# Half of the head pairs in swapped key order: three turnings instead of four per half, a mixing in smaller tiles, and the deviation put on the values by GpSimd

## The reference, cut to what matters

```python
h = tok(x)                                   # (128, 128, 128)
q, k, v = (layernorm(h) @ w + b for each)    # 8 heads of 64
logits = q @ k.T / 8, masked: key <= query   # 128 queries, 128 keys
h = h + softmax(logits) @ v @ wo + bo
h = h + routed_ffn(layernorm(h))             # top 2 of 8 experts
```

## Time and profile before

| | |
|---|---|
| median of 3 runs | 1257.07 us (1255.15 to 1257.45) |
| the profiled execution: its own time | 1256.33 us |
| its span from first to last instruction | 1254.6 us |
| work outside the span (1256.33 - 1254.6) | 1.7 us |
| busy: PE, DVE, ACT, POOL | 93%, 79%, 79%, 60% of the span |

### The profile page before, as it was taken

One profiled execution on the slowest core, in us unless ns is written; L12 is line 12 of the kernel. 1 busy time (PEld: TensorE's weight loads), 2 busy tenths in 40 slices (PEclk: granted clock), 3 DMA queues, 4 the chain that ended last, 5 costly groups with the idle time before them and its releaser, 6 DMA issues. The chain is left out here.

```text
span 1254.6 us, 45360 instructions
## 1 busy us (share of the span) xinstructions
PE 1172.8 (93%) x13125; PEld 1031.4 (82%) x13126; DVE 993.3 (79%) x3799; ACT 992.7 (79%) x3491; POOL 755.2 (60%) x1082
## 2 busy tenths in 40 slices
PE   6899999999999999999999999729999997999996
PEld 4578888888888888888888887619999996999995
DVE  6568988888888888888888887756777774777774
ACT  2799999999999999999999998726666664666663
POOL 6436755565565555565565555544777774777775
PEclk9899999999999999999999999968999998999998
DMA  5151110100100111110010111115666663555552
GB/s 177 60 186 56 39 35 32 43 32 32 47 32 32 43 36 32 42 37 32 32 43 32 36 43 40 53 53 170 197 206 199 203 191 130 159 143 143 159 153 68
DMA packets 68049, 108.97 MB, mean 87 GB/s; under 512 B 12756, under 2 KB 32948, under 8 KB 67860
## 3 DMA queue, kind: packets, MB, share of 16 engines
q1 hardware_dynamic: 50068, 62.67, 17.7%
q0 software_dynamic: 17920, 45.55, 10.0%
HBM read 45.66 MB, written 54.11 MB: 80 GB/s over the span
## 5 line engine op out<-in xcount | busy, mean ns | idle before, releaser
L764 ACT ACTIVATE probs<-ps,neg_max 128x128 f32<-128x128 f32 (+1 forms) x1024 | 337.8, 363 | 2.0 <-DVE neg_max L961 1.9
L764 ACT ACTIVATION_READ_ACCUMULATOR probs<-ps,neg_max 128x1 f32 x1024 | 236.3, 231 | 0.0
L574 POOL TENSOR_TENSOR probs<-probs,inv_sums 128x384 f32<-128x384 f32 x120 | 99.2, 826 | 205.4 <-DVE inv_sums L910 205.4
L1143 DVE SCALAR_TENSOR_TENSOR probsT<-ps,b_now,masked 128x256 f32<-128x256 f32 x286 | 125.3, 480 | 85.5 <-PE ps L1237 66.0
L1235 PE MATMUL ps<-xT_hi,w_now 128*128 128x256 f32 x572 | 173.1, 303 | 0.8 <-DVE xT_lo L1127 0.8
L720 ACT ACTIVATE masked<-ps,b_now 128x256 f32<-128x256 f32 x286 | 119.8, 471 | 59.5 <-PE ps L1237 59.1
L1237 PE MATMUL ps<-xT_hi,w_now 128*128 128x256 f32 x572 | 162.8, 285 | 0.0
L1236 PE MATMUL ps<-xT_lo,w_now 128*128 128x256 f32 x572 | 161.9, 283 | 0.0
L631 POOL DMA_INDIRECT xs<-normed,row x128 | 137.0, 1070 | 41.2 <-issue 36.9
L1418 PE MATMUL ps<-w,probsT 128*128 x1144 | 150.8, 275 | 0.0
L1363 PEld LDWEIGHTS ps<-probsT,v 128*64 128x64 f32 x2048 | 109.8, 137 | 45.2 <-issue 44.4
(11 more groups left out here) (243 smaller groups left out, 3181.8 us busy)
## 6 DMA issues: line engine op xcount, KB each, us to landing
v<-xs SPq DMA_DIRECT2D x108, 260.0 KB
kT<-xs SPq DMA_DIRECT2D x35, 260.0 KB
xs<-pad_rows SPq DMA_DIRECT2D x16, 520.0 KB, 3.4
normed<-h SPq DMA_DIRECT2D x32, 256.0 KB, 2.6
w_parts<-in_w SPq DMA_DIRECT2D x1, 2048.0 KB, 8.9
xs<-normed,row POOLq DMA_INDIRECT x128, 2.7
xs<-v POOLq DMA_INDIRECT x108
out_h<-v POOLq DMA_INDIRECT x108
```

Source lines behind the costliest of these rows:

```text
L764: ins = nc.scalar.activation(probs_p[par][:, half, slots[n]], ps[:, SCORES + half, slots[n]], ACT.Exp, bias=neg_max[par][:, half, n:n + 1] ...
L1143: V.scalar_tensor_tensor(actT[z][:, f], ps[:, H2[z], f * BLK:(f + 1) * BLK], b1_now[j % WBUFS][:, 2 + f:3 + f], gate[z][:, f], ALU.add, AL ...
```

## The change

1. `key`: ACT stores the keys of the odd pairs of heads with the two halves of each sequence exchanged (a negative step over halves in its read).
2. `scores`, `max`, `exp`: same number of products and columns; `slots` are moved, so that of a half's 384 columns every 128 are one full 128 x 128 block. The lower queries of an even pair sit beside those of an odd pair, whose lower keys are now "upper" ones: the one fills partitions 0 to 63, the other 64 to 127 after turning.
3. `probsT0`, `probsT1`: three turnings of 128 x 128 a half in place of four, and copies of 384 columns in place of 512, without a scale. `probsT1` gets a wait for `mixT_ready`, as its bank is now used by the mixing too. The zeros of L1149 are gone.
4. `mix`: 16 products of 64 columns: first 8 for the lower queries in tiles of 64 rows by 64 columns, then 8 for the upper ones in tiles of 128 rows by 64 columns; into two banks (3 and 4). ACT's copy reads both banks.
5. `value` (and the table for it, once): the odd pairs' values must stand in exchanged order too, so that the one product of 512 columns becomes one of 256 columns and two of 256 columns whose outputs are 64 partitions each.
6. A new step `vscale` on POOL multiplies the values of one sequence (128 x 512) in place by 1/deviation. DVE puts the exchanged copy of `rstd` beside it with two small copies at the end of `norm`. `rstd_now` and its copy are gone. The first mixing of a group waits for `v_scaled` in place of `v_ready`.

```diff
@@ octet_steps
         if octets_done == 0 and k == 0:
             steps.extend(("value", 0, n) for n in range(GB))
+            steps.extend(("vscale", 0, n) for n in range(GB))
...
             late("route_weight", half - 2)
+        steps.append(("vscale", half + 1, n))
         late("scatter", half - 3, n, n + 1)
@@ final_steps
-        steps += [*FINAL[k][0], ("scale0", k), *FINAL[k][1]]
+        steps += [*FINAL[k][0], ("scale0", k)]
+        if k < GB:
+            steps.append(("vscale", 1, k))
+        steps += FINAL[k][1]
@@ tiles
-        slots = (slice(0, S), slice(S + HQ, 2 * S + HQ), slice(S, S + HQ), slice(2 * S + HQ, PACK))
+        slots = (slice(0, S), slice(2 * S, PACK), slice(S, S + HQ), slice(S + HQ, 2 * S))
+        turned_at = (slice(0, S), slice(S, 2 * S), slice(2 * S, PACK))
@@ POOL
-                    pool.wait_ge(rstd_ready, LEAD + G + 1)
-                    pool.wait_ge(pTb_ready, LEAD + GB * (G - 1))
+                elif kind == "vscale":
+                    G, n = 2 * o + i, st[2]
+                    pool.wait_ge(v_ready, LEAD + GB * G + n + 1)
+                    pool.wait_ge(rstd_put, LEAD + 2 * (G + 1))
                     carry_wait(pool)
-                    pool.tensor_copy(rstd_now[i % 2][:], rstd[i % 2][:]).then_inc(rstd_put, 1)
+                    rows = v[i % 2][:, n].rearrange("p (c n d) -> p c n d", c=2, n=2)
+                    pool.tensor_tensor(rows, rows, rstd[i % 2][:, n].unsqueeze(1).broadcast_to([S, 2, 2]).unsqueeze(3).broadcast_to([S, 2, 2, 128]),
+                                       ALU.mult).then_inc(v_scaled, 1)
@@ ACT
-                        nc.scalar.activation(kT[par][:, pair], ps[:, KEY], ACT.Identity, bias=bias_qk[:, 1, pair:pair + 1],
-                                             scale=1.0).then_inc(qk_ready, 1)
+                        keys = ps[:, KEY].rearrange("p (j a c) -> p j a c", j=GB, a=2)
+                        nc.scalar.activation(kT[par][:, pair].rearrange("p (j a c) -> p j a c", j=GB, a=2), keys[:, :, ::-1] if pair % 2 else keys,
+                                             ACT.Identity, bias=bias_qk[:, 1, pair:pair + 1], scale=1.0).then_inc(qk_ready, 1)
...
-                    nc.scalar.activation(probsT[:, 4:8], ps[:, PROBST + 1].rearrange("p (n k) -> p n k", n=4), ACT.Identity,
-                                         scale=rstd_now[gp][:, j:j + 1]).then_inc(pTb_ready, 1)
+                    nc.scalar.copy(probsT[:, 4:7].rearrange("p n k -> p (n k)"), ps[:, PROBST + 1, 0:PACK]).then_inc(pTb_ready, 1)
...
-                    nc.scalar.copy(mixedT[:], ps[:, MIX]).then_inc(mixT_ready, 1)
+                    nc.scalar.copy(mixedT[:].rearrange("p (c n) q -> p n c q", n=2),
+                                   ps[:, MIX - 1:MIX + 1, 0:2 * S].rearrange("p n (c q) -> p n c q", c=2)).then_inc(mixT_ready, 1)
@@ DVE, norm
                     ins.then_inc(normed_ready, 1)
+                    dve.wait_ge(v_scaled, LEAD + GB * (G - 1))
+                    carry_wait(dve)
+                    for c in range(2):
+                        V.tensor_copy(rstd[par][(1 - c) * HQ:(2 - c) * HQ, :, 1], rstd[par][c * HQ:(c + 1) * HQ, :, 0]).then_inc(rstd_put, 1)
@@ PE
-                    T.matmul(ps[:, VALUE], onehot[par][:, j * S:(j + 1) * S], v_table[:], start=True, stop=True).then_inc(v_full, 1)
+                    T.matmul(by_pair(ps[:, VALUE])[:, :, 0], onehot[par][:, j * S:(j + 1) * S], by_pair(v_table[:])[:, :, 0], start=True, stop=True)
+                    for c in range(2):
+                        ins = T.matmul(by_pair(ps[(1 - c) * HQ:(2 - c) * HQ, VALUE])[:, :, 1], onehot[par][:, j * S + c * HQ:j * S + (c + 1) * HQ],
+                                       by_pair(v_table[:])[:, :, 1], start=True, stop=True)
+                    ins.then_inc(v_full, 1)
...
-                    for n in range(4):
-                        ins = T.transpose(turned(1, n), probs_p[par][:, 1, slots[n]], ident[:])
+                    for part in turned_at:
+                        ins = T.transpose(ps[:, PROBST + 1, part], probs_p[par][:, 1, part], ident[:])
...
-                        pe.wait_ge(v_ready, LEAD + GB * (2 * o + i // GB + 1))
+                        pe.wait_ge(v_scaled, LEAD + GB * (2 * o + i // GB + 1))
...
-                    for pair in range(PAIRS):
-                        for e in range(2):
-                            head = 2 * pair + e
-                            ins = T.matmul(ps[e * HD:(e + 1) * HD, MIX, pair * S:(pair + 1) * S], v[gp][:, j, head * HD:(head + 1) * HD],
-                                           probsT[:, e * PAIRS + pair], start=True, stop=True)
+                    for part in (1, 0):
+                        for c in range(2):
+                            for n in range(2):
+                                for e in range(2):
+                                    heads = slice((4 * c + 2 * n + e) * HD, (4 * c + 2 * n + e + 1) * HD)
+                                    keys, queries, at = ((slice(0, S), HQ, 2 * n), (slice(n * HQ, (n + 1) * HQ), 0, 1))[part]
+                                    ins = T.matmul(ps[e * HD:(e + 1) * HD, MIX - 1 + n, c * S + queries:c * S + queries + HQ], v[gp][keys, j, heads],
+                                                   probsT[keys, e * PAIRS + at, c * HQ:(c + 1) * HQ], start=True, stop=True)
```

More of the change, by code:

```diff
@@ L206, in build @@
         stats = sb("stats", [S, GB, 6]); moments = sb("moments", [S, GB, 2])
-        var_eps = sb("var_eps", [S, GB]); rstd = [sb(f"rstd{i}", [S, GB]) for i in range(2)]; rstd_now = [sb(f"rstd_now{i}", [S, GB]) for i in range(2)]; minus_half = sb("minus_half", [S, GB])
+        var_eps = sb("var_eps", [S, GB]); rstd = [sb(f"rstd{i}", [S, GB, 2]) for i in range(2)]; minus_half = sb("minus_half", [S, GB])
         normed = sb("normed", [S, GB, D])
@@ L242, in build @@
         sums = [sb(f"sums{i}", [S, 2, 4]) for i in range(2)]
-        inv_sums = [sb(f"inv_sums{i}", [S, 2, 6]) for i in range(2)]
+        inv_sums = [sb(f"inv_sums{i}", [S, 2, 8]) for i in range(2)]
         probs_p = [t[:].rearrange("p n k -> p (n k)")[:, 0:2 * PACK].rearrange("p (e c) -> p e c", e=2) for t in probs]
-        slots = (slice(0, S), slice(S + HQ, 2 * S + HQ), slice(S, S + HQ), slice(2 * S + HQ, PACK))
+        slots = (slice(0, S), slice(2 * S, PACK), slice(S, S + HQ), slice(S + HQ, 2 * S))
+        turned_at = (slice(0, S), slice(S, 2 * S), slice(2 * S, PACK))
         probsT = sb("probsT", [S, HEADS, S])
@@ L909, in invert @@
                 V.reciprocal(inverse[:, :, 0:2], sums[par][:, e, 0:2].unsqueeze(2).broadcast_to([S, 2, 2]))
-                return V.reciprocal(inverse[:, :, 2], sums[par][:, e, 2:4])
+                return V.reciprocal(inv_sums[par][:, e, 2:4], sums[par][:, e, 2:4])
             def step(o, st, opening=False, final=False):
@@ L981, in step @@
                     part = probs_p[par][:, 1].rearrange("p (n k) -> p n k", n=6)
-                    V.tensor_tensor(part, part, inv_sums[par][:, 1].unsqueeze(2).broadcast_to([S, 6, HQ]),
+                    V.tensor_tensor(part, part, inv_sums[par][:, 1, 0:6].unsqueeze(2).broadcast_to([S, 6, HQ]),
                                     ALU.mult).then_inc(scaled1, 1)
@@ L1237, in three, with by_pair @@
                 return T.matmul(dst, w_lo_, x_hi_, start=False, stop=True)
[L1239 to L1242 removed]
+            def by_pair(heads):
+                return heads.rearrange("p (c n d) -> p c n d", c=2, n=2)
             def step(o, st, opening=False, final=False):
@@ L1327, in step @@
                                 rows, pair = slice(e * HD, (e + 1) * HD), 2 * c + n % 2
+                                keys = slice(at, at + S) if high else slice(at + HQ * (n % 2), at + HQ * (n % 2) + HQ)
                                 ins = T.matmul(ps[c * HQ:(c + 1) * HQ, SCORES + e, slots[n]], qT[gp][rows, pair, at + high * HQ:at + high * HQ + HQ],
-                                               kT[gp][rows, pair, at:at + (S if high else HQ)], start=(n == 0), stop=False, skip_group_check=True)
+                                               kT[gp][rows, pair, keys], start=(n == 0), stop=False, skip_group_check=True)
                     for e in range(2):
                         rows = slice(e * HD, (e + 1) * HD)
-                        masked_keys = ps[:, SCORES + e, 0:PACK].rearrange("p (a k) -> p a k", a=2)[:, :, HQ:S + HQ]
-                        ins = T.matmul(masked_keys, ident_2[rows].rearrange("p c q -> p (c q)"), causal[rows].rearrange("p a n k -> p a (n k)"), start=False, stop=True,
+                        masked_keys = ps[:, SCORES + e, HQ:HQ + 2 * S]
+                        ins = T.matmul(masked_keys, ident_2[rows].rearrange("p c q -> p (c q)"), causal[rows].rearrange("p a n k -> p (a n k)"), start=False, stop=True,
                                        skip_group_check=True)
@@ L1336, in step @@
                 elif kind == "probsT0":
-                    if type(o) is int and b == 0:
```

(6 more changed lines are left out.)

39 lines of the change are left out of this document (19 added, 20 removed).

## The result

The changed kernel takes 1294.48 us (1293.53 to 1296.78, 4 runs); the kernel before takes 1257.26 us (1255.15 to 1257.49, 4 runs). The ratio is 1.030, with a 95% interval of 1.0285 to 1.0317. That is 37 us more, where I had forecast 22. The profiled execution took 1293.5 us and spans 1291.8.

The account below looks back on a forecast made before the run. PE was taken to set the pace, with ACT right behind at one step in four. PE's sum 0.00, 29 groups at +0.66 us make +19, last octet +2, cold start and octet 1 +1: 1279 us, range 1248 to 1300.

Parts of the forecast that it names:

- the dear rival: Mixing or POOL: short rounds don't pay, +0.4 us a sequence, or a longer `vscale` also catches L1073; 1290 to 1320, chance 0.13.
- signs named as wrong: Step 3's scores following mixing as closely as step 2's, L982 at 0.56 in that step, or a values step still 0.21.
- POOL's 0.17 us: POOL, step 1: time from L559's end to the next instruction, taken as the delay before `vscale` starts.
- My own interval, 298.63 to 299.73: POOL, step 1: when `vscale` would hold POOL, placed on the earlier trace, with L982 wanted at 299.06.
- the 0.78: DVE, step 1: lateness of L982, 0.53 us from the lock plus 0.25 from copies and wait; step 3's scores 0.66 later.
- The sign that I had named: Scores of step 3: distance from the mixing 0.8 us longer than in step 1, if the forecast is right.
- PE's own sum: PE, per sequence: turnings -0.22, mixing -0.04, values +0.26, together 0.00 us; bounds -0.40 to +0.4.
- ACT's copies: ACT: two copies lose 128 columns each, saving 0.08 us a copy, perhaps 0.12.
- my 3: Outside the regular groups: last octet +2 us, cold start and octet 1 together +1.
- The lock doesn't bite: DVE beside `vscale`: L982 not held, DVE late by 0.25 us alone; 1263, or 1257 to 1267, chance 0.15.
- The changes of shape are free: PE: new tile-shape changes cost nothing, -0.39 us a sequence; 1257 with full DVE delay, down to 1241; chance 0.16.
- Short rounds don't pay: Mixing: weights don't load behind 64 columns in tall tiles, +0.4 us a sequence; 1290 to 1320, dearer cases' chance 0.13.

Follow-up runs that it names:

- e7: Kernel before plus only a POOL multiplication of 128 x 512 by 1.0 in the places of `vscale`, with the mixing waiting for it: 1280.69 us.
- e1: Changed kernel with the `vscale` of step 1 of each half octet issued in step 2, beside that step's own: 1275.02 us.
- e8: Changed kernel with the two `rstd` copies at the very end of step 3 instead of the end of `norm`: 1281.56 us.
- e3: Changed kernel with the values in two products of full tiles, from a second one-hot with key halves exchanged: 1275.70 us.
- e9: Changed kernel with full-tile values, tall mixing tiles first, `rstd` copies ending step 3, step 1's `vscale` behind scatter: ratio 1.0088 to 1.0136, another chip.
- e4: Changed kernel with the mixing's two parts in the other order, tall tiles first: 1286.88 us.
- e10: As e9, but with the two `rstd` copies left at the end of `norm`: ratio 1.0245 to 1.0294, on the same other chip.

## Why the forecast was right, and where its sizes were off

- **How far it was right.** 1294.48 us lies in the range, 1248 to 1300, and the direction is the one forecast. But it is 37 us where 22 was the likeliest, and it lies in the band of the dear rival (1290 to 1320) too; it is within the range since the range took in half of that rival. One of the signs named as wrong is there, a `scale1` at 0.56 in that step, and another nearly so, scores of step 3 that follow the mixing as closely as those of step 2.
- **The cause holds**: `vscale` in step 1 locks DVE out, DVE is late with its chain, PE waits once a group, and the change is slower by that. e7 shows the hold alone (+24 us), e1 takes it away alone (-19.5).
- **Where the lock bites was wrong.** The forecast put it on L982 (`scale1`). L995 is as fast as ever, and the four pieces of L1086 are held instead, by 0.69 (forecast for `scale1`: 0.53). I had that version only among the dear rivals. The step that failed is the timing of `vscale`: I took POOL's 0.17 us ahead of a transfer's issue to hold for `vscale` too, but L609 starts at 335.44, 0.02 before L565's record ends, and 0.08 before the fourth piece. My own interval, 298.63 to 299.73, already overlapped the last piece of L1073, which ends at 297.16 + 1.72 = 298.88; I compared it with L982 alone. That piece starts at 298.52, 0.11 ahead of the interval, so that 0.17 us decided which of the two came first.
- **The two copies** were put at 0.25, bounds 0.1 to 0.4; they measured 0.51 (e8: 0.52). I had priced them by the reciprocals. L958 shows 0.36 for the two, and `route_apply` follows them by 0.17 us where it followed the norm by 0.05.
- **What is late next.** I let the 0.78 arrive at the scores of step 3, over the exponentials. The exponentials did start when the maxima end (338.25 and 338.28), but PE had already stopped for L980, whose bank the turning of the normed group needs. Before, L980's counterpart had some 0.3 us in hand; of 1.21 us of lateness 0.90 arrived. The sign that I had named, 0.8 us between mixing and scores, is not there: it is 1.11 against 1.01 in step 2.
- **PE's own sum** was put at 0.00 a sequence and is +0.08, as in the first two steps of the table (+0.07, +0.08). Turnings -0.22; mixing 1.01 for 1.03, -0.02 (forecast -0.04); values 0.43 for 0.21, +0.22 (forecast +0.26); `project` 1.03 for 0.93, +0.10, not in the forecast. The last is the first round after the half tiles: e3 takes it back, 0.92.
- **ACT's copies** gained more than forecast, 0.69 to 0.48 for half 0's, -0.21 for -0.08, and the time of the kernel shows nothing of it, since ACT is not what the long step waits for.
- **The sum.** 29 long steps at 0.99 instead of 0.66 make 10 us, 29 groups with +0.13 to +0.19 from the other three steps make 5: 22 + 15 = 37, as measured. That the ends still come to my 3 is chance: the last octet costs 4.8 us (first scores to last, 50.6 for 45.8) where I had 2, and what follows it is 2.1 shorter in this trace (441.8 for 443.9). There half 0's scaling, L988, is held once through two GpSimd instructions in a row and ends 0.42 after the second:

```profile
830.32 1.04 POOL L609 TENSOR_TENSOR v<-v,rstd 128x512 f32<-128x512 f32 x1
831.32 1.33 POOL L601 TENSOR_TENSOR residual<-h,bias_o 128x544 f32<-128x544 f32 x1
830.41 2.66 DVE L988 TENSOR_TENSOR probs<-probs,inv_sums 128x384 f32<-128x384 f32 x1
```

- **The rivals.** "The lock doesn't bite" falls with e7. "The changes of shape are free" falls with e3, which gains 19 us by taking two of them away. "Short rounds don't pay" falls with the mixing's 1.01.

The Trainium skill (SBUF — State Buffer, section "SBUF: two separate sides") gives the lock to a DVE instruction in a two-port mode as well as to one with two SBUF inputs, whichever engine starts first holding it for a whole instruction. L1086, with one input, held by L580 and by L609, agrees as far as what is locked goes; no row names its mode. On who is first, records differ from it: the second piece of L1086 starts at 334.41, 0.03 before L580, and is held for 0.94 us all the same, and in e9 L1002 starts 0.65 us before `vscale`, is the first therefore, and would have been through at 308.08.

The Trainium skill (TensorEngine Tiling (Array Packing), section "Key Properties") says that a change of tiling mode drains TensorE. e3 and e4 agree and give its price here: 0.31 us for two changes and the round behind them, and 0.12 from mixing to scores for one.

## What to carry to other kernels

Before an instruction goes on GpSimd, lay its interval over VectorE's timeline and ask which instructions between SBUF and SBUF it will meet, those with one input too; then look at the place behind it, for a hold that is avoided on one row may land on the next. Cheap work on a late engine costs what stands behind it: put it where nothing that another engine waits for follows in the same step. A saving on TensorE pays only in the steps that TensorE sets; in e3 and e4 the long step kept its length or grew. And where a run misses its expectation in one place alone, look at the granted clock there before you look for another wait.

## What was not expected of the hardware

- Two VectorE copies of 64 x 4 elements, 0.36 us in the timeline, lengthen the chain by 0.51, with their wait.
- GpSimd seems to hold the shared way before its record begins. In the earlier trace rows `scale1` starts 0.43 us into the transfer's issue and takes 0.56; in e9 it starts 0.43 into it as well, with `vscale` next in GpSimd's queue instead of an instruction that has to wait for `scale1`, and takes 2.13. The last octet of the changed kernel shows besides that a waiting VectorE instruction isn't let in between two GpSimd instructions in a row. The records alone don't tell when the hold began, and no run here separates it further.
- TensorE's granted clock can fall because of a wait that another engine causes: in e10, after waits of 1.8 us in one step, 3.4 us at 0.50 cost 1.27 us more. Half 1 of the same octets, with the same waits, kept 1.00.
- After products in tiles of 64 columns the first row of full tiles behind them is slower as well: `project` 1.03 instead of 0.92.
